# A five-layer graph network: two of 62 edge columns by single-row transfers from SyncE and ScalarE instead of one from SyncE

## The reference, cut to what matters

```python
# CONV1, CONV2 (8 relations, 4 heads) and GAT (1 relation, 1 head), for each edge:
alpha = leaky_relu(qn[etype, dst] + kn[etype, src])
ex = exp(alpha - segment_max(alpha, dst)[dst])
out = segment_sum(ex / denom[dst] * xw[etype, src], dst)
# RGCN (8 relations), for each edge:
out = segment_sum(edge_weight * xw[etype, src], dst)
# GINE: relu(h[src] + edge_attr), summed over edges, then a small MLP
```

## Time and profile before

| what | value |
|---|---|
| median of 3 runs | 22680.64 us |
| the profiled execution, span from its first to its last instruction | 22678.7 us |
| busy: POOL, VectorE, ScalarE, TensorE | 16413.3, 10606.0, 5421.1, 5315.0 us |
| instructions | 201879 |
| single-row DMAs by SyncE | 26624 |
| gathers by POOL in the four layers | 12688 |

### The profile page before, as it was taken

The page is one execution under the profiler, slowest core; times in us unless marked ns, Lnnn a source line. Parts: engine busy times, 40 slices in busy tenths (PEclk is TensorE's granted clock), DMA queues, the critical chain, the costliest instruction groups (busy, mean ns, idle before and its releaser), DMA issues.

```text
span 22678.7 us, 201879 instructions
## 1 busy us (share of the span) xinstructions
PE 5315.0 (23%) x30665; PEld 3876.7 (17%) x30665; DVE 10606.0 (47%) x9480; ACT 5421.1 (24%) x4707; POOL 16413.3 (72%) x17069
## 2 busy tenths in 40 slices
PE   2000000020000001222222266666662222222201
PEld 1000000010000001222222255555552000000001
DVE  2444444324444443556566668888884111111167
ACT  1222222222222222111111132222221211121175
POOL 7777777677777776777777767777776777777733
PEclk9999999999999999666666655555555666666655
DMA  6333333332222222222222232222222222222164
GB/s 203 95 98 101 95 98 98 88 97 76 70 75 70 72 73 46 54 54 58 54 57 55 52 87 56 52 56 52 56 52 61 84 76 76 76 80 80 66 235 162
DMA packets 782414, 1839.84 MB, mean 81 GB/s; under 512 B 380834, under 2 KB 415306, under 8 KB 720302
## 3 DMA queue, kind: packets, MB, share of 16 engines
q0 software_dynamic: 544128, 569.36, 13.8%
q10 hardware_dynamic: 88736, 721.35, 8.1%
q1 hardware_dynamic: 148622, 541.43, 6.7%
HBM read 1007.43 MB, written 929.12 MB: 85 GB/s over the span
## 4 chain that ended last, share of the span: by engine, by line
POOL 55%; issue 24%; SPq 12%; DMA 3%; DVE 2%; PE 2%; ACT 1%; POOLq 0%; DVEq 0%; ACTq 0%
POOL region L652 41%; POOL by_src L742 12%; SPq L615 9%; SPq L613 3%; DMA region<-by_src 2%; DMA row_list<-row_lists 1%; POOL q_rel L713 1%; SPq L614 1%; PE ps L1207 1%; DVE region L1567 1%; DVE region L1538 0%; PE ps L1168 0%; POOL h_edge L725 0%; PE ps L1209 0%; POOL q_one L713 0%
## 5 line engine op out<-in xcount | busy, mean ns | idle before, releaser
L652 POOL DMA_INDIRECT region<-table,idx x12688 | 11972.1, 944 | 3941.9 <-issue 3873.2
L742 POOL DMA_INDIRECT by_src<-region,idx x3224 | 3122.7, 969 | 1007.9 <-issue 1001.5
L1950 DVE TENSOR_TENSOR region<-ps,region 128x248 f32<-128x248 f32 (+1 forms) x156 | 74.4, 477 | 3958.0 <-DMA region<-table,idx 1967.5
L1216 PE MATMUL ps<-ident,region 128*68 128x128 f32 (+1 forms) x3 | 1.3, 444 | 8044.9 <-DVE region L2013 8044.9
L1767 DVE TENSOR_TENSOR region<-ps,region 128x2048 bf16<-128x2048 f32 x833 | 1845.8, 2216 | 18.2 <-DVE region L1761 8.0
L870 ACT COPY region<-region 128x4216 f32<-128x4216 f32 (+1 forms) x156 | 1182.2, 7579 | 2477.7 <-DVE region L1996 2477.7
L1112 PE MATMUL ps<-region 98*128 98x128 f32 x6448 | 1657.9, 438 | 323.3 <-DVEq L1833 192.8
L1533 DVE CAST region<-src 128x62 f32 (+1 forms) x52 | 11.7, 224 | 3463.8 <-DMA by_src<-region,idx 3463.6
L1207 PE MATMUL ps<-region,ident 128*128 128x512 f32 (+1 forms) x832 | 809.5, 1062 | 3141.2 <-DVE region L1538 3141.2
L1112 PEld LDWEIGHTS ps<-region 98*128 98x128 f32 x6448 | 1455.9, 330 | 410.7 <-DVEq L1833 269.7
L1905 DVE TENSOR_TENSOR_SCAN region<-region,ps 128x1008 f32<-128x1008 f32 x624 | 1382.9, 2244 | 10.7
(11 more groups left out here) (291 smaller groups left out, 16216.1 us busy)
## 6 DMA issues: line engine op xcount, KB each, us to landing
sums<-region ACTq DMA_DIRECT2D x104, 2232.0 KB
region<-table SPq DMA_DIRECT2D x13312, 0.3 KB
sums<-region ACTq DMA_DIRECT2D x104, 1984.0 KB, 11.1
region<-table,idx POOLq DMA_INDIRECT x12688
region<-table SPq DMA_DIRECT2D x6656, 0.3 KB
region<-table SPq DMA_DIRECT2D x6656, 0.2 KB
sums<-region ACTq DMA_DIRECT2D x52, 2046.0 KB
region<-by_src SPq DMA_DIRECT2D x52, 2015.0 KB, 9.6
```

Source lines behind the costliest of these rows:

```text
L652: pool.indirect_dma_start(out=to, out_offset=None, in_=table, in_offset=bass.IndirectOffsetOnAxis(ap=index, axis=0)).then_inc(s, 16)
L742: pool.indirect_dma_start(out=by_src, out_offset=bass.IndirectOffsetOnAxis(ap=idx[:, b, j:j + 1], axis=0), in_=MSG[:, b, j, :], in_offset= ...
```

## The change

ROWED = 2 columns of each chunk are fetched row by row, so POOL gathers 60 columns. Of the 256 rows SyncE takes 160 and ScalarE 96. The registers loaded at a time (RUN) are 32. The lists of row numbers are made three times at the start, multiplied by the row's size in bytes (for the tables of 68, 65 and 64 numbers), and the DMA's source is the table as bytes, from that offset. ScalarE asks for its part of the next chunk's list at the chunk's start; in the score layers it issues 64 rows for the next chunk after L900's copy and 32 after the exponentials, in RGCN eight after each of the first 12 quads. The zeros for h_edge are written in quarters of a chunk, one for each chunk of each of the four layers. The semaphores for the rows are five for each half, shared by the layers and cleared by VectorE between them. The diff, cut to its core:

```diff
@@ -62,8 +63,14 @@
 J1 = J + 1
 PIECES = 4
 PF = D // PIECES
-JP = J - 1
-RUN = 16
+ROWED = 2
+JP = J - ROWED
+RUN = 32
+ROWS = ROWED * P
+SP_ROWS = 160
+ROW_GROUPS = [(0, 64), (64, 128), (128, 160), (160, 224), (224, 256)]
+ROW_KIND = {0: 0, 1: 0, 2: 1, 3: 2}
+QUARTERS = 4
 assert HI * LO == NP and NG % 2 == 0 and NQ == 2 * NG and GROUP == 2 * QUAD and FARTHER > NP
...
 
+        lists = wide[0:CH].rearrange("p a b -> p (a b)").bitcast(I32)
+        list_src, list_type = lists[:, 0:ROWS], lists[:, ROWS:2 * ROWS]
+
+        def row_place(l, b, k):
+            p, j = divmod(k, ROWED)
+            return slots(l)[1][p:p + 1, b, 1 + JP + j, :].bitcast(U8)
+
+        def row_bytes(l, at):
+            n = 4 * row_in(l)
+            return tables[l].bitcast(U8).rearrange("n f -> (n f)")[bass.ds(at, n)].unsqueeze(0)
+
+        def row_group(k):
+            return [lo <= k < hi for lo, hi in ROW_GROUPS].index(True)
+
         block = ctx.enter_context(nc.Block())
...
 
-            sp.dma_start(row_list[:, 1, :], a["src"].rearrange("(p c j) -> c p j", p=P, c=CH)[:, :, J - 1]).then_inc(loaded, 16)
-            sp.dma_start(row_list[:, 0, :],
-                         a["edge_type_8"].rearrange("(p c j) -> c p j", p=P, c=CH)[:, :, J - 1]).then_inc(loaded, 16)
+            sp.dma_start(list_src.rearrange("c (p j) -> c p j", p=P),
+                         a["src"].rearrange("(p c j) -> c p j", p=P, c=CH)[:, :, JP:J]).then_inc(loaded, 16)
...
             sp.dma_start(dst_f.rearrange("(p s) k -> p (s k)", p=P), dst_v).then_inc(idx_dram, 16)
             sp.dma_start(sub_last, sub_v).then_inc(idx_dram, 16)
             sp.wait_ge(lists_ready, 1)
-            sp.dma_start(row_lists[0:CH, :], row_list[:, 0, :]).then_inc(list_in, 16)
-            sp.dma_start(row_lists[CH:2 * CH, :], row_list[:, 1, :]).then_inc(list_in, 16)
+            sp.dma_start(row_lists[0:CH, :], row_list[:, :]).then_inc(list_in, 16)
...
+                    sp.wait_ge(list_in, 48)
                 with sp.Fori(0, CH // 2) as i:
                     for b in range(2):
-                        sp.dma_start(row_list[0:1, b, :], row_lists[bass.ds(i * 2 + (kind + b), 1), :]).then_inc(list_in, 16)
+                        sp.dma_start(row_list[b:b + 1, 0:SP_ROWS],
+                                     row_lists[bass.ds(i * 2 + (CH * ROW_KIND[l] + b), 1), 0:SP_ROWS]).then_inc(list_in, 16)
                         sp.wait_ge(idx_ready, i * 2 + ((CH + 2) * l + b + 1))
                         sp.sem_inc(chunk_begun, 1)
-                        sp.wait_ge(list_in, i * 32 + 16 * (CH * l + b + 3))
+                        sp.wait_ge(list_in, i * 32 + 16 * (CH * l + b + 4))
                         sp.sem_inc(chunk_begun, 1)
-                        for p0 in range(0, P, RUN):
-                            sp.load(indices, row_list[0:1, b, p0:p0 + RUN])
+                        for k0 in range(0, SP_ROWS, RUN):
+                            sp.load(indices, row_list[b:b + 1, k0:k0 + RUN])
                             for k, row in enumerate([sp.snap(r) for r in indices]):
-                                sp.dma_start(G[p0 + k:p0 + k + 1, b, J, :],
-                                             tables[l][bass.ds(row, 1), :]).then_inc(rows_in[l][b][2 * p0 // P], 16)
-                        if l == CONV1:
...
+                def ask_rows(i, b):
+                    act.dma_start(row_list[b:b + 1, SP_ROWS:ROWS],
+                                  row_lists[bass.ds(i * 2 + (CH * ROW_KIND[l] + b), 1), SP_ROWS:ROWS]).then_inc(act_list_in, 16)
+
+                def rows_begin(i, b):
+                    act.wait_ge(idx_ready, i * 2 + ((CH + 2) * l + b + 1))
+                    act.sem_inc(chunk_begun, 1)
+                    act.wait_ge(act_list_in, i * 32 + 16 * (CH * l + b + 1))
+                    act.sem_inc(chunk_begun, 1)
+
+                def fetch_rows(b, k0, n):
+                    act.load(act_indices[0:n], row_list[b:b + 1, k0:k0 + n])
+                    for k, row in enumerate([act.snap(r) for r in act_indices[0:n]]):
+                        act.dma_start(row_place(l, b, k0 + k), row_bytes(l, row)).then_inc(rows_in[b][row_group(k0 + k)], 16)
+
+                def fetch_all(i, b):
+                    rows_begin(i, b)
+                    for k0 in range(SP_ROWS, ROWS, RUN):
+                        fetch_rows(b, k0, RUN)
+
+                if l in SUMMED:
+                    for q in range(GP):
+                        act.wait_ge(stored[q], 16 * TURNS * (l + 1))
+                    if l == CONV1:
+                        act.wait_ge(list_in, 48)
+
                 def send_sums(i, b, O):
                     act.wait_ge(sum_ready, i * 2 + (CH * l + b + 1))
                     act.dma_start(sum_rows[:, bass.ds(i * (2 * J) + b * J, J), :], O).then_inc(sum_out, 16)
...
+                    ask_rows(0, 0)
+                    fetch_all(0, 0)
+
                     def score_chunk(i, b, more):
                         nth = CH * l + b + 1
                         at = i * (2 * J) + b * J
+                        if more:
+                            ask_rows(i + b if b else i, 1 - b)
                         act.wait_ge(e_in, i * 32 + 16 * nth)
                         act.copy(EQT, EQ.rearrange("p j k -> p k j")).then_inc(e_read, 1)
                         if more:
                             act.wait_ge(e_read, i * 2 + nth)
                             act.dma_start(q_to, q_rows[:, bass.ds(i * (2 * w) + (b + 1) * w, w)]).then_inc(e_in, 16)
                         act.copy(REP[:, 0:k, 1:J1], bc(cont[:, bass.ds(at, J)], 1, k)).then_inc(q_in, 1)
+                        if more:
+                            rows_begin(i + b if b else i, 1 - b)
+                            for k0 in range(SP_ROWS, ROWS - RUN, RUN):
+                                fetch_rows(1 - b, k0, RUN)
                         act.wait_ge(ex_in, i * 2 + nth)
                         if l == GAT:
                             act.activation(REP.rearrange("p (h f) j -> p h f j", h=h), bc(EX[:, 0], 2, D // h),
@@ -907,6 +964,8 @@
                         if l != GAT:
                             act.activation(REP.rearrange("p (h f) j -> p h f j", h=h), bc(EX[:, 0], 2, D // h),
                                            ACT.Exp).then_inc(rep_in, 1)
+                        if more:
+                            fetch_rows(1 - b, ROWS - RUN, RUN)
                         store_sums(i, b, O)
                         send_sums(i, b, O)
...
                     def finish_chunk(i, b, ranks):
+                        if ranks:
+                            ask_rows(i + b if b else i, 1 - b)
                         for n in range(NQ):
                             if ranks:
                                 copy_turned(i + b if b else i, 1 - b, n)
+                                if n == 0:
+                                    rows_begin(i + b if b else i, 1 - b)
+                                if n < (ROWS - SP_ROWS) // 8:
+                                    fetch_rows(1 - b, SP_ROWS + 8 * n, 8)
                             if n in (4, 8, 12):
                                 finish_piece(i, b, n // 4 - 1)
                         finish_piece(i, b, PIECES - 1)
                         send_sums(i, b, O)
 
+                    ask_rows(0, 0)
+                    fetch_all(0, 0)
                     for n in range(NQ):
                         copy_turned(0, 0, n)
...
-            stt(out=row_list[:, 0, :], in0=row_list[:, 1, :], scalar=float(REL), in1=row_list[:, 0, :], op0=ALU.mult,
-                op1=ALU.add).then_inc(lists_ready, 1)
+            done(stt(out=list_type, in0=list_src, scalar=float(REL), in1=list_type, op0=ALU.mult, op1=ALU.add))
+            settle()
+            done(ts_(row_list[:, :], list_type, 4.0 * row_in(CONV1), None, ALU.mult))
+            done(ts_(list_src, list_src, 4.0 * row_in(GAT), None, ALU.mult))
+            settle()
+            ts_(list_type, list_type, 4.0 * row_in(RGCN), None, ALU.mult).then_inc(lists_ready, 1)
...
                                 dve.wait_ge(gathered[l][b], i * (16 * JP) + 16 * JP)
-                                for half in range(2):
-                                    dve.wait_ge(rows_in[l][b][half], i * (8 * P) + 8 * P)
+                                for part, (lo, hi) in enumerate(ROW_GROUPS):
+                                    dve.wait_ge(rows_in[b][part], i * (16 * (hi - lo)) + 16 * (hi - lo))
```

More of the change, by code:

```diff
@@ L10 @@
 BF16 = mybir.dt.bfloat16
+U8 = mybir.dt.uint8
 ACT = mybir.ActivationFunctionType
@@ L333, in build @@
         list_in = sem("list_in")
-        rows_in = {l: [[sem(f"rows_in{l}_{b}_{k}") for k in range(2)] for b in range(2)] for l in SUMMED}
+        rows_in = [[sem(f"rows_in{b}_{k}") for k in range(len(ROW_GROUPS))] for b in range(2)]
+        act_list_in = sem("act_list_in")
         dst_ready = sem("dst_ready")
@@ L598, in _ @@
                     sp.dma_start(q_to, q_rows[:, 0:w]).then_inc(e_in, 16)
```

(27 more changed lines are left out.)

11 lines of the change are left out of this document (7 added, 4 removed).

## The result

The changed kernel takes **22748.47 us** (median of 6 runs, 22745.84 to 22754.92) against 22674.81 (6 runs, 22672.05 to 22682.27) before: a ratio of **1.0032 [1.0021, 1.0044]**, 0.3% slower. The profiled execution spans 22744.1 us where before's spans 22678.7, so 65.4 us are to be found.

A forecast was written before the change was run, and what follows sets the result against it. SyncE was to bound all four stages: -0.6 us x 52 chunks in CONV1 and 78.0 - 76.2 over 156 others, -31 + 281 = +250 us on the span of 22678.7, giving 22,930 us, 1.1% slower; range 22,340 to 23,400.

The forecast's parts named there:

- POOL's saving: POOL gathers 60 columns instead of 61: 74.9 us a chunk, 1.3 less; -330 us if nothing else bound.
- SyncE bounds the score layers: SyncE's chunk, 76.8 us in CONV1 and 78.0 behind it, exceeds POOL's 74.9, so SyncE would bound all four stages.
- The cheaper row: SyncE's row without the multiplication saves 0.076 us: 0.320 in CONV1, 0.332 behind it; 160 rows take 53.1 us.
- A load of 32 with its copies: SyncE's five batches: load 2.3 us, twice an undisturbed load of 16, plus 0.86 of copies; 15.8 us a chunk instead of 13.4.
- list, zero rows and loop's edge: SyncE's chunk behind CONV1: 2.6 us for list fetch and loop's edge, 0.7 for issuing zero rows, 1.15 for the later list.
- delays: SyncE's rows and loads behind ScalarE's stores: 4.6 us a chunk, taken over from CONV2 before the change.
- ScalarE's part: ScalarE's list, loads and rows hidden: cost 0 at the lower row price, up to 150 us in RGCN at the upper.
- The prediction's last check: Among the signs of what would show it: RGCN alone above the other stages would be ScalarE's price.
- Rival 1: SyncE's load of 32 is far below twice that of 16; at 1.24 us POOL binds, 22,350 us; chance 0.36.
- Rival 2: SyncE and ScalarE disturb each other issuing rows; 0.05 us for each of ScalarE's 96 rows gives 23,930 us; chance 0.07.
- Rival 3: The errors cancel: SyncE at 76.6 to 77.0 us behind CONV1, time within 0.2% of before; chance 0.10.
- Rival 4: SyncE's row gets no cheaper because the byte offset needs its own operation: 12 us a chunk more, 25,460 us; chance 0.02.

The follow-up runs named there:

- the ninth kernel: Changed kernel with SyncE 152 rows, ScalarE 104; in RGCN ScalarE's list asked for before the store, no rows beside finished pieces: 22397.89 us, 0.9878 of the kernel before.
- experiment 3: Changed kernel with SyncE writing h_edge's zero rows whole in CONV1 alone, not in quarters in every stage: ratio 1.0043 to the kernel before.
- experiment 1: Changed kernel without ScalarE's list, loads and single rows, so 96 rows a chunk are not fetched and sums are wrong: ratio 0.9891 to the kernel before.
- experiment 5: Changed kernel with ScalarE's list in RGCN asked for before the last piece's copy and the store of the sums: ratio 0.9954 to the kernel before.
- the tenth kernel: Changed kernel, still 160 and 96 rows, with RGCN's list asked for early and no rows beside a finished piece: ratio 0.9958 to the kernel before.

## Why the direction came true by luck and the size did not

- **POOL's saving** (60 gathers, 74.9 us a chunk) was right, and the ninth kernel collects it: the prediction's -330 us for "nothing else bound" stands against 0.0122 x 22,676 = 277 measured. Most of the difference is RGCN, 28 us shorter than before where 67 were expected.
- **SyncE bounds the score layers**: right, by the chain. The forecast of its chunk was 76.8 in CONV1 (measured 76.0) and 78.0 behind it (76.6 and 75.4). **Two terms were too large.** The cheaper row was put at 0.332 us behind CONV1 and 0.320 in it; it is 0.318 and 0.312, since the multiplication and its gaps were worth 0.090 in CONV2 (0.084 in CONV1) and not 0.076: 160 x 0.014 = 2.2 us. A load of 32 with its copies was put at 3.16 and is 2.94 (2.13 of it the load, put at 2.3): 1.1 us over five. Against that stand 0.8 us more of list, zero rows and loop's edge (5.3 where 2.6 + 0.7 + 1.15 were summed) and 1.2 more of delays: 5.8 for 4.6, if all that lies above the usual row and load is counted and not only the clearly late ones of above. 78.0 - 2.2 - 1.1 + 0.8 + 1.2 = 76.7, CONV2's number to 0.1.
- **GAT was given CONV2's row.** It has 0.312 and not 0.318, another 1.0 us, 75.4. The trace before could not have told this, since its median is 0.408 in both layers; and in experiment 3 GAT has 0.318.
- **The step that failed: ScalarE's part was costed at 0 and cost RGCN 3.6 us a chunk** (187 us, experiment 1). The prediction: "ScalarE's list DMA, the loop's edge that its longer body may now show" and others are "hidden or once per layer: 0, at most 30 us"; and "at quads 4 and 8 ScalarE is late by some 3 us each", "DVE has 9.2 us before L1854", "Cost 0 at the lower price". The 9.2 are there and ScalarE's price was the lower one, but the sum on them is 11.3 us: 1.5 and 1.3 at the quads, half of what was said, and 8.4 at the start of the chunk, which was not said at all. The list behind ScalarE's own 2 MB store is 3.0 of these 8.4 (experiment 5). The prediction priced SyncE's list behind SyncE's own write (6.5 us) and did not ask what stands ahead of ScalarE's list. The other 5.4 come with the first rows behind the store and the loop's turn, 5.3 us in every second chunk, and are not taken apart. The prediction's last check, "RGCN alone above the others would be ScalarE's price", is what happened.
- **Sum.** Against before the forecast had -31 us in CONV1 and +94 in each other layer; measured are -77, +16, -47 and +167. It is 46 + 78 + 141 = 265 us too high in the score layers and 73 too low in RGCN, where the cause is not in its sum: together 192 of the 182 us by which the forecast was missed.
- **The direction is luck.** The forecast was slower because SyncE would bind. Where SyncE alone binds, the change is faster: the three score layers together gained 107.5 us, and the tenth kernel, with SyncE's chain in all four layers, has the ratio 0.9958. The changed kernel is slower only by RGCN's 167 us, of which none was in the sum for ScalarE.
- **Rival 1** (a load far under twice that of 16) had the sign's threshold at 2.06 us. The load came out at 2.13, at the forecast's side by 0.07 us, and the sign of the score layers still came out as the rival's, since the row was cheaper too. Loads of 16 and 32 registers take 1.23 and 2.13 us here, which is 0.33 us and 0.056 for each register; a load of 8 takes 0.73, 0.05 below that line. By the Trainium skill (DMA: Bandwidth & Descriptors, "Latency and other measured facts") a load has a floor of some 600 ns, from which the prediction had an estimate of 1.88 us; the trace's fixed part is about half of that. The rule of 200 ns a register in the Trainium skill (Runtime: NRT & Kernel Launch, "Instruction fetch mechanics") would have given 6.4 us and is not borne out by these loads from SBUF.
- **Rival 2** (the queues disturb each other) exists at a tenth to a fifth of its price: 0.005 to 0.011 us a row. **Rival 3** (SyncE at 76.6 to 77.0, within 0.2% of before) had the chunk nearly right, 76.6 and 75.4, and not the layer that spoilt it. **Rival 4** is out: no FUSED_REGOPS between the rows.

## What to carry to other kernels

Work moved to an idle engine costs nothing only if the sum of all that it adds to one chunk fits into the slack of the chain that waits for it, and each small DMA that the engine then waits for has to be priced by what stands ahead of it in its queue. A list for the next round should be asked for ahead of the large store of this round, a change of one line that turned +0.3% into -0.5% here. Two kernels of the same length need not have the same bound: the fifth and the tenth have an RGCN of 3997 and 3998 us, the one held by ScalarE and VectorE, the other by SyncE, and only the chain and the waits told. Where two engines are balanced within 2%, a sum whose terms are good to 1 us a chunk can't give the sign; measure its smallest units per stage, and try the split of the work, since 160 and 96 rows lost what 152 and 104, in better places, won.
